# First LayerNorm's row scaling moved from VectorE to ScalarE, its statistics split around the second norm, and a table load moved, in a transformer block kernel

## The reference

```python
def reference(x, ctx, ...):                    # x 4 x 2048 x 512, ctx 4 x 154 x 512, all fp32
    x = x + xattn(layernorm(x), ctx, ctx)      # first norm: (x - mean) / sqrt(var + 1e-5)
    x = x + ffn(layernorm(x))
    return x

def xattn(q, k, v):                            # 16 heads of 32, 8 key/value heads
    q1, q2 = split(q @ Wq.T); k1, k2 = split(k @ Wk.T); vh = v @ Wv.T
    w = softmax(q1 @ k1.T) - lam * softmax(q2 @ k2.T)
    attn = w @ vh                              # then RMS norm, g, factor 1 - LAMBDA_INIT
    return attn @ Wo.T

def ffn(x):                                    # hidden 2048
    h = gelu(layer_norm(x, ln1_g, ln1_b) @ ternary(w1).T + b1)
    return layer_norm(h, ln2_g, ln2_b) @ ternary(w2).T + b2
```

## Time and profile before

| what | value |
|---|---|
| median of 3 runs | 2423.88 us (2423.76 to 2427.24) |
| the profiled execution | 2423.49 us, its span 2421.5 us |
| mean granted TensorE clock | 0.983 |
| busy: PE, DVE, ACT, POOL | 2286.6, 1714.2, 1339.7, 993.4 us |
| busy shares of the span | 94%, 71%, 55%, 41% |
| last chain of waits | PE 70%, DVE 17%, DMA, ACT, POOL and issue 3% each |

### The profile page before, as it was taken

The page is one execution under the profiler, slowest core; times in us unless marked ns, Lnnn a source line. Parts: engine busy times, 40 slices in busy tenths (PEclk is TensorE's granted clock), DMA queues, the critical chain, the costliest instruction groups (busy, mean ns, idle before and its releaser), DMA issues.

```text
span 2421.5 us, 35774 instructions
## 1 busy us (share of the span) xinstructions
PE 2286.6 (94%) x13791; PEld 1083.1 (45%) x13791; DVE 1714.2 (71%) x2701; ACT 1339.7 (55%) x1945; POOL 993.4 (41%) x807
## 2 busy tenths in 40 slices
PE   8679999999999999999989999999999999999978
PEld 5344534445353544535344454534445453544433
DVE  4677768686785868678676867868676786867663
ACT  3435655556465555656555555655556565555544
POOL 0102625436172534627153452715346271534517
PEclk9779999999999999999999999999999999999989
DMA  7412103030210303021130302112040211203000
GB/s 262 120 25 62 27 24 83 15 92 15 78 30 29 78 15 92 15 66 27 43 79 15 92 15 66 28 47 59 15 107 15 66 28 50 56 15 75 15 22 18
DMA packets 105661, 125.88 MB, mean 52 GB/s; under 512 B 22512, under 2 KB 74284, under 8 KB 104980
## 3 DMA queue, kind: packets, MB, share of 16 engines
q1 hardware_dynamic: 105492, 123.60, 18.4%
HBM read 51.80 MB, written 20.36 MB: 30 GB/s over the span
## 4 chain that ended last, share of the span: by engine, by line
PE 70%; DVE 17%; DMA 3%; ACT 3%; POOL 3%; issue 3%; SPq 1%; POOLq 0%; ACTq 0%; DVEq 0%
PE ps L1421 16%; PE ps L1443 9%; PE ps L1433 9%; PE ps L1319 5%; PE ps L1366 5%; PE ps L1344 4%; PE ps L1264 4%; PE ps L1373 4%; PE ps L1265 3%; PE ps L1266 3%; DVE attn_raw L993 2%; DVE arena L1052 2%; DVE arena L941 2%; DMA arena<-in_x 2%; DVE arena L955 2%
## 5 line engine op out<-in xcount | busy, mean ns | idle before, releaser
L563 POOL TENSOR_TENSOR attn_raw<-attn_raw 128x512 f32<-128x512 f32 x448 | 579.1, 1311 | 153.5 <-ACT attn_raw L720 146.2
L1421 PE MATMUL ps<-rows,w1T 128*128 128x512 f16 x2048 | 486.9, 381 | 24.8 <-DVE rows L1047 24.8
L955 DVE TENSOR_REDUCE arena<-ps 128x3 f32<-128x462 f32 (+1 forms) x704 | 413.0, 618 | 111.0 <-PE ps L1319 110.1
L529 POOL TENSOR_TENSOR q<-q 128x512 f16<-128x512 f32 x128 | 158.3, 1241 | 723.3 <-ACT q L666 706.6
L715 ACT ACTIVATE attn_raw<-ps,vec_cols,wstep 128x512 f32<-128x512 f32 x256 | 198.7, 776 | 276.3 <-PE ps L1421 274.4
L1052 DVE SCALAR_TENSOR_TENSOR arena<-attn_raw,vec_cols,arena 128x512 f16<-128x512 f32 x256 | 231.8, 905 | 86.1 <-ACT arena L718 84.5
L1421 PEld LDWEIGHTS ps<-rows,w1T 128*128 128x128 f16 x2048 | 191.8, 98 | 222.1 <-DVE rows L1047 38.0
L1443 PE MATMUL ps<-w2T,arena 128*128 128x512 f16 x1088 | 271.2, 379 | 0.0
L686 ACT ACTIVATE arena<-ps 128x1024 f32<-128x1024 f32 x128 | 131.6, 1028 | 228.3 <-PE ps L1344 228.3
L975 DVE SCALAR_TENSOR_TENSOR p<-arena,p 128x512 f16<-128x512 f32 x128 | 88.1, 688 | 236.7 <-ACT p L690 236.7
L1319 PE MATMUL ps<-k_att,stack_raw 96*128 96x154 f16 x2048 | 222.0, 233 | 27.2 <-DVE arena L955 25.2
(11 more groups left out here) (183 smaller groups left out, 3478.7 us busy)
## 6 DMA issues: line engine op xcount, KB each, us to landing
stack_raw<-q SPq DMA_DIRECT2D x768, 64.0 KB, 2.0
arena<-in_x SPq DMA_DIRECT2D x64, 256.0 KB, 2.7
out<-arena SPq DMA_DIRECT2D x64, 256.0 KB, 2.1
arena<-in_x SPq DMA_DIRECT2D x15, 1024.0 KB, 6.2
arena<-in_L_ffn_w SPq DMA_DIRECT2D x7, 1024.0 KB, 10.1
stack_raw<-in_L_xattn_Wq SPq DMA_DIRECT2D x8, 256.0 KB, 5.8
k_att<-k_store SPq DMA_DIRECT2D x4, 490.0 KB
k_store<-attn_raw SPq DMA_DIRECT2D x12, 160.0 KB
```

Source lines behind the costliest of these rows:

```text
L563: ins = pool.tensor_tensor(acc[:, e, :], acc[:, e, :], src[:, j % NG, :], ALU.add)
L955: dve.tensor_reduce(negmax[:, tt, u0:u1], ps[:, row_bank(c, tb), 0:(u1 - u0) * S].rearrange("p (u s) -> p u s", s=S), AX.X, ALU.max, negat ...
L1421: ins = pe.matmul(ps[:, B_H + j % 2, :], w1T[:, k, j * P:(j + 1) * P], rows16[:, e, k, :], start=(k == 0 and e == 0), stop=(k == KD - 1 an ...
```

## The change

It moves four pieces of work and adds one small one. The arithmetic of the first norm's rows is written as `rstd * x + offset` instead of `(x - mean) * rstd`.

```diff
+LN1_ROWS_AT = {2: (0,), 3: (1,), 4: (2,), 5: (3,)}
...
+        offset1 = sb("offset1", [P, TT], F32)
...
@@ gpsimd, iteration
                 power(1, s_var2, s_rstd2, i)
-                if ahead2:
-                    power(0, s_var1, s_rstd1, i + 2)
                 power_half(i, 0)
                 if ahead:
                     q_lo(i + 1, QATT)
                 power_half(i, 1)
                 wait(pool, s_xhat2, i, TT, TT)
+                if ahead2:
+                    power(0, s_var1, s_rstd1, i + 2)
...
@@ scalar
+            def ln1_rows(c, tts):
+
+                wait(act, s_off1, c - 2, 1, 1)
+                for tt in tts:
+                    act.activation(x_in[:, tt, :], x_in[:, tt, :], ACT.Identity, bias=offset1[:, tt:tt + 1],
+                                   scale=rstd[:, 0, tt:tt + 1]).then_inc(s_xhat1, 1)
...
@@ scalar, iteration
+                load_table(ACT.Gelu)
                 if ahead:
                     for n in range(QATT, QEARLY):
                         q_hi(i + 1, n)
-                load_table(ACT.Gelu)
                 h_hi(i)
...
                 for j in range(JH):
                     gelu(i, j)
+                    if ahead2 and j in LN1_ROWS_AT:
+                        ln1_rows(i + 2, LN1_ROWS_AT[j])
...
@@ vector
-            def ln1_stats(c):
+            def ln1_stats(c, tts=range(TT)):
                 wait(dve, s_xin, c, 16, 16)
-                for tt in range(TT):
+                for tt in tts:
                     ins = dve.bn_stats(stats[:, 0, tt, :], (x_in if c else x_in0)[:, tt, :])
+                if tts[-1] < TT - 1:
+                    return
                 ins.then_inc(s_st1, 1)
...
+            def ln1_offsets(c):
+
+                wait(dve, s_rstd1, c, 1, 1)
+                dve.scalar_tensor_tensor(offset1[:], mv[:, 0, :, 0], -1.0, rstd[:, 0, :], ALU.mult,
+                                         ALU.mult).then_inc(s_off1, 1)
...
-            def mid_rows(c):
+            def mid_rows(c, ahead2):
 
                 wait(dve, s_rms, c, 1, 1)
                 dve.tensor_scalar(var[:, 1, :], ps[:, B_O, 0:TT], 1.0 / D, EPS, ALU.mult, ALU.add).then_inc(s_var2, 1)
+                if ahead2:
+                    ln1_stats(c + 2, (0, 1))
                 wait(dve, s_rstd2, c, 1, 1)
...
@@ vector, iteration
+                mid_rows(i, ahead2)
                 if ahead2:
-                    ln1_stats(i + 2)
-                mid_rows(i)
+                    ln1_stats(i + 2, (2, 3))
+                h_lo(i)
                 if ahead2:
-                    ln1_rows(i + 2)
-                h_lo(i)
+                    ln1_offsets(i + 2)
```

More of the change, by code:

```diff
@@ L286, in build @@
             "ln1_stats", "ln1_aggr", "ln1_var", "ln1_rstd", "ln1_rows"))
+        s_off1 = sem("ln1_offsets")
         s_xt, s_xt_hi, s_xt_lo = sem("x_transposed"), sem("x_hi"), sem("x_lo")
```

## The result

The changed kernel takes 2391.67 us in the median of 4 runs (2389.21 to 2392.57), the kernel before 2425.56 us in 4 runs beside it: ratio 0.9862, with a 95% interval of 0.985 to 0.9874. The profiled execution has a span of 2387.2 us, 34.3 less than before. Run again, it took 2389.76 us in the median of 5, ratio 0.9851 (0.9838 to 0.9864).

The account below looks back on a forecast made before the run. VectorE's chain ahead of hidden step 0 was taken as the bound. Gap 25.0 plus late transfers 8.6 less ScalarE's rows 1.4 gave 32.2 us off 2423.5, forecast as 2391.5 us, range 2386 to 2397 (60%).

Parts of the forecast that it names:

- The bound: Ahead of hidden step 0, once per block: VectorE's chain to `h_lo`, mostly hidden by query products; cutting 3.5 us wins at most 1.7.
- The gap: TensorE's wait ahead of hidden step 0: 1.73 us per block closes, 25.0 us in total.
- The charge of 0.1 us per block for the row behind step 2: ScalarE's row instruction behind Gelu 2 delays Gelu 3 by 0 to 0.2 us, taken as 0.1; 1.4 us over 14 blocks.
- the prediction's sign of a wrong forecast: TensorE's waits for row maxima (L975): a longer total than before would show the forecast wrong.
- The margin: Ahead of hidden step 0: VectorE's and ScalarE's chains both end 0.2 us before TensorE is ready.
- Late transfers: Waits at query products and second norm's transposes, 8.4 + 2.2 us, less 1.3 and 0.7 left over: 8.6 us won.
- the 0.5 us that the prediction named as a sign of being wrong: A wait before hidden step 0 of over 0.5 us would show the forecast wrong, its releaser telling which chain is late.
- Copy 7: ScalarE's query copy 7, behind GpSimd's low half 5, ends at 1092.6, 0.1 us before hidden step 0 ends; Gelu 0 isn't delayed.
- The margin wasn't lost: Rival, 18%: ahead of hidden step 0 `h_lo` starts 0.5 to 1.2 us later, or Gelu 0 is held up; 2402 us.
- the late transfers were mostly won back: Rival, 8%: the block load's wait stands inside the second norm's chain, so 8.6 us are not won back; 2400 us.
- relief reached the row maxima: Rival, 5%: VectorE's relief halves TensorE's 25.2 us of waits for row maxima at L1319; 2379 us.
- slower: Rival, 4%: ScalarE becomes the bound in hidden steps 2 to 5, its row instructions passing through at 44 us; 2434 us.

## Why the prediction was right, point by point

The forecast was 2391.5 us, measured were 2391.67 and 2389.76. That it fits to 0.2 us is partly luck. The forecast was worked out from the profiled execution of the kernel before, 2423.49 us, less 32.2; the profiled execution of the changed kernel took 2389.21, 34.3 less. So the gain was forecast 2 us too small, and the median of the kernel before, beside which this was measured, was 2425.56 instead of 2423.88. The last step of the sum has a slip as well: 2391.3 and 0.4 are 2391.7.

Where the gain comes from can be read at hidden step 0 of block 15, which started at 2350.11 us. Now it is 34.4 us earlier:

```profile
2315.70 9.85 PE L1443 MATMUL ps<-rows,w1T 128*128 128x512 f16 x32 [2.23 <-DVE rows L1069]
```

Blocks 0 to 13, each taken at the 1.85 us of a steady one, make 25.9, and block 14 makes 0.7 (the distance ahead of its step 0 falls from 0.92 to 0.22 us): 26.6 us. The rest, 7.8 us, belongs to late transfers.

**The bound.** One chain on VectorE that TensorE's query products almost cover: right. The rows alone gave 1.11 us per block, the table load alone nothing, and all together 1.85, so ScalarE's chain lay hidden behind VectorE's as their rows had shown.

**The gap.** Forecast 25.0 us less 1.4 for ScalarE's rows, 23.6; measured 26.6. Two sizes were off. The charge of 0.1 us per block for the row behind step 2 was close to nothing: putting it later won nothing. And a steady block won 1.85 us, not the 1.73 of the gap from start to start. The rest of it stands in rows of both traces: the transposes take 1.91 instead of 1.99 us and hidden step 0 1.89 instead of 1.92, since the matmuls within these runs start closer together. The waits for row maxima went from 0.95 to 1.04 us in block 6 and stayed at 0.95 in block 5, so the prediction's sign of a wrong forecast, a longer total of them, did come, but with 0.3 us.

**The margin.** Forecast 0.2 us for both chains, and that the forecast hangs on it. In 12 of the 15 blocks with query products hidden step 0 starts 0.21 or 0.22 us after the matmul ahead of it, so there it held. ScalarE's chain is the tighter: in block 6 step 0 starts 1077.31 - 1074.92 = 2.39 us after `h_hi`, which needs 2.18, a margin of 0.21 us as forecast. VectorE's is about 0.45, since the two statistics between L1027 and L1031 cost nothing where 0.1 was counted, and the pause in block 6 is that block's alone. In blocks 3, 7 and 11 the margin was lost.

**Late transfers.** Forecast 8.6 us, measured 7.8, for a partly wrong reason. I had left 1.3 us in block 7 and 0.7 in one other, through the load of the block. VectorE now waits for it at most 0.62 us. What is left is 2.0, 1.0 and 1.3 us ahead of hidden step 0 in blocks 3, 7 and 11, over the 0.5 us that the prediction named as a sign of being wrong, and comes from another transfer. ScalarE in block 3 of the changed kernel:

```profile
652.54 0.60 ACT L667 ACTIVATE q<-ps 128x512 f32<-128x512 f32 x1 [5.54 <-DMA stack_raw<-q]
...
660.13 0.60 ACT L667 ACTIVATE q<-ps 128x512 f32<-128x512 f32 x1 [4.35 <-DMA stack_raw<-q]
```

Query copy 6 waits for the transfer that empties its buffer and holds up `h_hi` behind it; copy 6 of blocks 7 and 11 waits 3.55 and 3.60 us in the same way. Why these transfers are late is open: the run with the values load moved gave no clear answer. Before, the mid rows were later still and covered it. So 4.4 us of waits are left where 2.0 were forecast, and the total still comes out only 0.8 us short, because the 10.6 us that went were worth more: each of the ten waits is listed about 0.16 us shorter than what it costs from start to start, 1.6 us in all, which the prediction added for the gap and not here.

**GpSimd.** Copy 7 was to end 0.1 us ahead of need. In block 6 it ended 0.1 us after: Gelu 0 started at 1079.33, and hidden step 0 had ended at 1077.31 + 1.89 = 1079.20. Nothing came of it.

**The rivals.** The margin wasn't lost in the steady blocks, the late transfers were mostly won back, and no relief reached the row maxima. For "slower", ScalarE's row instruction took 0.80 us, above my upper bound of 0.78, and none of it came through. The estimate from the Trainium skill (ScalarE: Activation LUTs, What ACT_TABLE_LOAD costs, on pointers and elements), 0.80 us, is the measured one. The drain that the Trainium skill gives in the same section isn't in this trace either: from L739 at 1061.55 to the end of its small instruction at 1062.85 + 0.20 are 1.5 us.

## What to carry to other kernels

Where two chains end close together, moving the shorter one alone shows nothing and becomes worth something once the longer is gone (here 0.75 us per block, of the 1.42 that the load takes); try such edits together, and undo each from the combined kernel to see its share. Read the margin off several blocks, not one, and for each chain, and measure it by adding an instruction of known length and looking at the distance of two blocks, which shows 0.2 us where the median of the runs doesn't. Before moving work to another engine, try it on the same engine behind the instruction that others wait for: here, with the other edits in place, that gave 1.40 of 1.85 us per block.

## What the runs showed of the hardware that I had not expected

VectorE instructions with two inputs in SBUF wait for a GpSimd instruction on 128x512 numbers that is already running. Of the changed kernel's 256 GELU low halves, the 205 that start while GpSimd is idle take 0.75 us, also where GpSimd begins beside them. The 51 that start while a GpSimd instruction runs take up to 1.85 us, and nearly all end 0.55 us after that instruction. With half of GpSimd's sums the mean falls from 906 to 798 ns. The offset instruction on 128x4 numbers takes 0.15 us in the three blocks where it starts beside an idle GpSimd and 0.65 or 0.86 in the others: in block 6 it starts at 1078.35 and ends at 1079.21, just after this pair on GpSimd (1076.92 + 2.27 = 1079.19).

```profile
1076.92 2.27 POOL L532 TENSOR_TENSOR q<-q 128x512 f16<-128x512 f32 x2
```

The first norm's rows of the kernel before (L941), fp32 with one tensor from SBUF and two columns of numbers, do the same: 36 took 0.53 or 0.54 us, and the 28 that started beside a running GpSimd instruction 1.37 or 1.38. The 0.9 us each of the prediction was a mean of both. Beside GpSimd's power on 128x2 numbers the same kind of instruction isn't slowed: 16 of the second norm's rows (L1041) start while one runs, and take 0.54 us. The statistics (L925), with one input, took 0.67 to 0.70 us either way.

The Trainium skill (GPSIMD Engine Reference, Specifications) says that GpSimd's SBUF interfaces are shared with VectorE, with contention for instructions that have two SBUF inputs or run in a two-port mode. For two inputs this case agrees, by the numbers above; whether the rows run in such a mode no run here shows.
